# One state-space layer and one attention layer with experts: three orders of work changed, two routings put beside other work

## The reference, cut to what matters

```
xn = layernorm(x)
x  = x + mamba(xn) + one_of_8_experts(xn)          # layer 0
xn = layernorm(x)
x  = x + attention(xn) + two_of_8_experts(xn)      # layer 1
```

```
dt = softplus(dt + dt_bias);  A = -exp(A_log)
L[i,j] = exp(sum of A*dt over j < k <= i), lower triangle only      # the decays within a chunk
y_diag  = (C B^T * L) (x*dt)                                        # within a chunk
S[c+1]  = decay(c) * S[c] + B^T (x*dt*decay to the end of the chunk) # states from chunk to chunk
y_off   = C S[c] * decay from the chunk's start
```

## Time and profile before

| | us |
|---|---|
| median of 3 runs (lowest, highest) | 2052.54 (2051.96, 2064.46) |
| the profiled execution's own time | 2049.56 |
| its span | 2047.8 |
| norm0 | 0 to 49.4 |
| route0 | 50.6 to 69.1 |
| time_steps | 70.1 to 93.3 |
| mamba, before its loop | 94.2 to 133.6 |
| mamba, loop | 133.6 to 716.3 |
| one_expert_each | 720 to 1029 |
| norm1 | 1029.2 to 1092.4 |
| route1 | 1093.6 to 1118.1 |
| project | 1119.1 to 1216 |
| attend_and_experts | 1219 to 2047.8 |

### The profile page before, as it was taken

The page is one execution under the profiler, slowest core; times in us unless marked ns, Lnnn a source line. Parts: engine busy times, 40 slices in busy tenths (PEclk is TensorE's granted clock), DMA queues, the critical chain, the costliest instruction groups (busy, mean ns, idle before and its releaser), DMA issues. The chain is left out here.

```text
span 2047.8 us, 33896 instructions
## 1 busy us (share of the span) xinstructions
PE 1803.0 (88%) x10070; PEld 1240.1 (61%) x10070; DVE 1381.2 (67%) x3090; ACT 1159.0 (57%) x2806; POOL 432.4 (21%) x406
## 2 busy tenths in 40 slices
PE   5389999999999889999844988999999898999998
PEld 2247657656766679999812454555556464656555
DVE  5648678768677612222165869798879888888885
ACT  2145665665565412222111538888888888888886
POOL 2004413422432334321110111020201002020101
PEclk9689899899899889999966999999999999999999
DMA  4412212312221188655173583252424333343311
GB/s 165 137 55 93 92 63 79 105 61 72 92 72 62 42 300 276 201 180 173 54 236 117 159 260 106 73 104 73 104 73 93 63 83 94 83 93 83 86 29 32
DMA packets 143790, 226.12 MB, mean 110 GB/s; under 512 B 17725, under 2 KB 110015, under 8 KB 143648
## 3 DMA queue, kind: packets, MB, share of 16 engines
q1 hardware_dynamic: 124464, 179.95, 29.1%
q0 software_dynamic: 19184, 44.45, 8.5%
HBM read 174.26 MB, written 50.99 MB: 110 GB/s over the span
## 5 line engine op out<-in xcount | busy, mean ns | idle before, releaser
L2286 DVE TENSOR_SCALAR att_scores<-att_psS 128x512 f32<-128x512 f32 x512 | 352.9, 690 | 95.3 <-PE att_psS L2116 94.8
L2235 ACT ACTIVATE att_prob<-att_scores,att_shift 128x512 f32<-128x512 f32 x512 | 383.2, 748 | 23.0 <-DVE att_shift L2302 22.9
L2244 ACT COPY att_pT<-att_psT 128x512 f32<-128x512 f32 x512 | 306.4, 599 | 132.5 <-PE att_psT L2124 131.9
L2294 DVE CUSTOM_DVE_ANT_0 att_scores<-att_scores,first_decay 128x512 f32<-128x512 f32 x512 | 352.0, 688 | 0.0
L2124 PEld LDWEIGHTS att_psT<-ident,att_prob 128*128 128x128 f32 x2048 | 244.8, 142 | 158.7 <-issue 97.6
L2124 PE MATMUL att_psT<-ident,att_prob 128*128 128x128 f32 x2048 | 315.1, 277 | 15.4 <-ACT att_pT L2244 14.8
L2116 PE MATMUL att_psS<-first_ks,first_qs 128*128 128x512 bf16 x512 | 195.8, 384 | 17.3 <-DVE att_scores L2286 13.5
L1123 ACT ACTIVATE mamba_L<-mamba_am,mamba_minus 128x128 f32<-128x128 f32 x512 | 153.9, 387 | 44.5 <-PE mamba_psY L998 44.4
L2138 PE MATMUL att_psO<-att_pT,att_v 128*32 128x512 f32 x1024 | 140.6, 624 | 37.8 <-ACT att_pT L2244 37.8
L1543 ACT ACTIVATE ffn_hT<-ffn_psH,ffn_b 128x128 f32<-128x128 f32 x156 | 44.7, 369 | 194.6 <-PE ffn_psH L1499 194.6
L1499 PEld LDWEIGHTS ffn_psH<-ffn_xT,ffn_w 128*128 128x128 f32 x1248 | 145.3, 192 | 3.6 <-DMA ffn_w<-in_w 0.9
(11 more groups left out here) (287 smaller groups left out, 2872.4 us busy)
## 6 DMA issues: line engine op xcount, KB each, us to landing
ffn_w<-in_w SPq DMA_DIRECT2D x39, 1024.0 KB, 5.6
mamba_am<-a_rows SPq DMA_DIRECT2D x64, 512.0 KB, 3.8
first_qs<-q_parts SPq DMA_DIRECT2D x256, 64.0 KB, 3.1
first_ks<-k_parts SPq DMA_DIRECT2D x256, 64.0 KB, 3.1
xn<-xn_all SPq DMA_DIRECT2D x16, 512.0 KB, 5.7
ffn_w<-in_w POOLq DMA_DIRECT2D x8, 1024.0 KB, 6.7
att_w<-in_inter POOLq DMA_DIRECT2D x7, 1024.0 KB, 5.5
att_w<-in_outer POOLq DMA_DIRECT2D x7, 1024.0 KB, 7.3
```

Of the source, the lines that this page charges most:

```text
L2235: nc.scalar.activation(prob[:, n % NP], scores[:, n % NCL], ACT.Exp, bias=shift[:, h % 2, t:t + 1], accum_out=total[:, octet % 2, t, j, i: ...
L2244: nc.scalar.copy(pT[:, h % HEADS_T, :, t * P:(t + 1) * P], bank_of("turn", n)[:].rearrange("p (k q) -> p k q", k=CPB)).then_inc(pT_ready, 1)
L2286: vec.tensor_scalar(scores[:, n % NCL], psS[n % NS][:], -CLAMP, CLAMP, ALU.max, ALU.min).then_inc(clipped, 1)
L2294: vec.tensor_tensor_reduce(scores[:, n % NCL], scores[:, n % NCL], decay[:, FAR - t * P:FAR - t * P + SEQ], 1.0, -2.0 * CLAMP, ALU.mult, A ...
```

## The change

Four things are changed.

1. **The mamba batch.** DVE's order was decays(0), grow(0), decays(1), grow(1), `fd`, grow(2). It is now grow(0), grow(1), decays(0), `fd`, grow(2), decays(1).
2. **The first table.** Its first two quarters are no longer multiplied ahead of the convolutions; each of the four stands behind a pair of convolutions. `keep_running` has 26 instead of 16 products.
3. **Both routings beside other work.** `route` becomes a class, `Router`, with its pieces as methods. In layer 0 it is merged with `time_steps` into one stage, `route_and_steps`; PE's order has the ranks first, and SP's has the bias and the 8 row stores ahead of `a_rows`. In layer 1 its pieces are spread over the sequences of `project`: b=0 the softmax and the first pick, b=1 the second pick, b=2 the mask (`choose`), b=3 the ranks taken up and `passes`, b=4 both slots and the first one-hot columns, b=5 the second columns and the first one-hot rows, then two quarters of rows per sequence, and the last ones behind the last sequence. On PE the ranks stand behind values(2), one table quarter behind values(6) and seven at the end. The second pick's one-hot rows reuse the first's buffer (semaphore `used`). The latent has one PSUM bank instead of two, so latent(b) waits for ACT's copy of b - 1, which keys(b - 1) ahead of it on PE waits for already.
4. **Row stores of layer 1.** `normalise` stores `xn1` on SP, each sequence behind its store to `out`.

```
-                    decays(0)
                     grow(0)
-                    decays(1)
                     grow(1)
+                    decays(0)
                     dve.wait_ge(fd_done, (i + 1) * CPB)
                     dve.wait_ge(xfd_ready, i * CPB)
                     v.tensor_tensor(fd[:], fd_ps, ...).then_inc(fd_ready, 1)
                     grow(2)
+                    decays(1)
...
-                keep_running(nc, C, psO[0][:, 0:P], 16)
-                for q in range(2):
-                    table.multiply(nc, pe, psP, 0, q)
+                keep_running(nc, C, psO[0][:, 0:P], 26)
...
                 for n in range(CT):
                     conv(0, n, False)
-                    if n in (3, 5):
-                        table.multiply(nc, pe, psP, 0, (n + 1) // 2)
+                    if n % 2 == 1:
+                        table.multiply(nc, pe, psP, 0, n // 2)
...
# normalise, SP
                         sp.dma_start(rows(merge[2], b), x[:, b]).then_inc(x_kept, 16)
+                        sp.wait_ge(xn_ready, (b + 1) * CPB)
+                        sp.dma_start(rows(xn_d, b), xn_all[:, b * CPB:(b + 1) * CPB, :]).then_inc(xn_kept, 16)
...
# route_and_steps, DVE
                 v.scalar_tensor_tensor(out=mag[:], ...).then_inc(mag_ready, 1)
+                router.chained(dve)
+                router.shift(dve)
                 dve.wait_ge(exped, 2)
                 v.tensor_scalar(w[:], u[:], 1.0, None, ALU.add).then_inc(w_ready, 1)
+                router.probabilities(dve)
+                router.pick(dve, 0)
+                router.choose(dve)
                 dve.wait_ge(w_ready, 1)
...
                            op0=ALU.mult, op1=ALU.mult).then_inc(a_ready, 1)
+                router.rank_all(dve)
+                router.tiles_of(dve)
+                router.first_slots(dve)
                 dve.wait_ge(decay_ready, 1)
...
# project, SP
                 sp.dma_start(wuv[:], w["wuv"]).then_inc(w_in, 16)
+                router.load(sp)
                 first.load_wo(sp)
# project, PE
                 def latent(b):
-                    if b >= 2:
-                        pe.wait_ge(lat_ready, b - 1)
+                    pe.wait_ge(lat_ready, b)
...
                     values(b)
-                pe.wait_ge(lat_ready, BATCH - 1)
-                for k in range(2):
-                    for q in range(4):
-                        table.multiply(nc, pe, psL[0][:, 0:2 * table.columns], k, q)
+                    if b == 2:
+                        router.ranks(pe)
+                    elif b == BATCH - 2:
+                        table.multiply(nc, pe, psR[:, 0:2 * table.columns], 0, 0)
+                for q in range(1, 4):
+                    table.multiply(nc, pe, psR[:, 0:2 * table.columns], 0, q)
+                for q in range(4):
+                    table.multiply(nc, pe, psR[:, 0:2 * table.columns], 1, q)
# project, DVE
                 v.tensor_tensor(wkT[:], wkT[:], wvT[:], ALU.add).then_inc(joined, 1)
+                router.chained(dve)
+                router.shift(dve)
                 dve.wait_ge(wkv_made, 1)
...
                         take_low(Q, b - 1)
+                    if b == 1:
+                        router.pick(dve, 1)
+                    elif b == 3:
+                        router.rank_all(dve)
+                    elif b == 4:
+                        router.second_slots(dve, 0)
+                    elif b == 5:
+                        table.columns_hot(nc, dve, choice, 1)
+                    elif b > 5:
+                        quarter = 2 * (b - 5) - 1
+                        table.rows_hot(nc, dve, choice, quarter // 4, quarter % 4)
                     if b < BATCH:
                         take(K, b)
                         subtract(Q, b)
                     if b:
                         take_low(K, b - 1)
-                    if b < 2:
-                        table.columns_hot(nc, dve, choice, b)
-                    if b < BATCH:
-                        table.rows_hot(nc, dve, choice, b // 4, b % 4)
-                table.take(nc, dve, psL[0], places)
+                    if b == 0:
+                        router.probabilities(dve)
+                        router.pick(dve, 0)
+                    elif b == 2:
+                        router.choose(dve)
+                    elif b == 3:
+                        router.passes(dve)
+                    elif b == 4:
+                        router.second_slots(dve, 1)
+                        table.columns_hot(nc, dve, choice, 0)
+                    elif b > 4:
+                        quarter = 2 * (b - 5)
+                        table.rows_hot(nc, dve, choice, quarter // 4, quarter % 4)
+                table.rows_hot(nc, dve, choice, 1, 3)
+                table.take(nc, dve, psR, places)
```

354 lines of the change are left out of this document (190 added, 164 removed).

## The result

Four runs of the changed kernel have a median of 2028.93 us (2023.86 to 2032.48), against 2053.05 for the kernel before: ratio 0.9858, 95% interval 0.9826 to 0.989. That is 24 us faster where I had forecast 57, and above my range. The kernel before moved too, from 2053.05 beside the first set to between 2038.02 and 2041.68 beside the others, so only the ratios compare across sets, and these two agree within their intervals. The profiled execution took 2028.95, its span is 2026.6.

What follows compares the result with a forecast made beforehand. Mamba's loop was taken as bound by PE, busy 550.4 of 582.7 us at mean clock 0.94, gaining where PE waits. Terms 28 + 13 + 4.5 + 11.5 = 57 off 2049.56 gave 1992.6, plus 3.0: 1995.5 us, range 1976 to 2023.

Steps and rivals of the forecast that it cites:

- The mamba batch: Mamba loop: DVE's earlier copies remove PE's 2.88 us wait per sequence and the low clock behind it; -28 (-10 to -38).
- the sign of being wrong that I had named: Mamba loop: a PE wait before diagonal(1) of 2 us or more would show the prediction wrong.
- Rival A: Mamba: lead lost between DVE and POOL, L(1) late, PE waits some 3 us, clock falls later; -4 to -16; chance 0.25.
- Route0 and time_steps: Layer 0's two short stages merged: DVE's chain ends at 79.9 instead of 93.3; -13 (-11 to -14).
- The first table: Mamba's start: table quarters between pairs of convolutions, last convolution ending at 121.6 instead of 126.06; -4.5 (-2 to -7).
- the lower end that I had named: First table at mamba's start: only -2 if the weights land late and PE idles into the low clock.
- Layer 1: Layer 1's routing stage goes (-25.5), row stores hide in norm1, project gets 14 longer; -11.5.
- project's lengthening: Project: router pieces on DVE, the later bias and shift, and low clock after PE's idle 3.1 add +14 (+10 to +19).
- Rival C: Layer 1 gives nothing back: project grows by 25, DVE waiting for PE in sequences 5 to 7; time 2007; chance 0.13.
- all good ends together: Whole kernel: every step at its best gives -73, 1979.
- the forecast: The forecast's own case: mamba -20 to -38 and layer 1 -6 to -15; chance 0.55.
- Rivals B and D: B: slower, PE idles in mamba's dense part, 2055 to 2075, chance 0.04. D: copies not earlier, mamba 0, 2023, chance 0.03.

Runs made afterwards that it cites:

- pool_quiet: Changed kernel with POOL's products beside the third growth and first decays cut to one head of eight: 2004.66 us (one run), mamba loop 562.9.
- wait_filled: Changed kernel with eight products without use on PE behind diagonal(0), filling its wait for L(1): 1993.04 us, ratio 0.9767 to the kernel before, loop 545.9.
- again: The changed kernel run once more, unaltered: 2009.19 us, ratio 0.9836 to the kernel before.
- ranks_later: Changed kernel with PE's ranks in project behind queries(3) instead of values(2): 2004.26 us, ratio 0.9807 to the kernel before, project 115.7.
- table_warm: Changed kernel with 6 and 12 products without use filling PE's waits ahead of project's last table quarters: 2006.51 us, ratio 0.9819 to the kernel before.
- grow2_last: Changed kernel with DVE's order grow(0), grow(1), fd, decays(0), decays(1), grow(2): 2005.93 us, ratio 0.9824 to the kernel before, loop 558.9.
- no_wait: grow2_last with POOL's xdt(1) ahead of xfd(0): 2007.40 us, ratio 0.9815 to the kernel before, loop 557.4.
- skip_v2: Changed kernel with PE's skip matmuls of tile 1 moved between diagonal(0) and diagonal(1): 2018.69 us, ratio 0.989 to the kernel before, loop 563.8.
- skip_v1: no_wait with PE's skip matmuls of tile 1 moved behind diagonal(1), ahead of its state product: 2007.82 us, ratio 0.9846 to the kernel before, loop 559.1.

## Why the prediction was wrong

**The mamba batch, forecast -28, measured -13: this step failed.** Its first half was right: the wait of 2.88 went, PE made its second growth 3 us sooner. The second half read "waits about 0.7 for L(1)" and added "if it stays at full clock". The wait was 2.1 (0.5 to 0.7 by my own times), the sign of being wrong that I had named. PE came to diagonal(0) when I had said, 15.0 behind `near` for 15.2. But L(1) came at 19.1, not at 17.6, of which the stretch beside POOL is 1.3 (1.17 and 1.03 for 0.68 each, 1.71 for 1.23; pool_quiet took back the last two). And I took it that a wait so short would not touch the clock, with no row to show it. Rival A had this: L(1) late, PE waiting before diagonal(1), the clock falling "as before, only later", mamba -4 to -16. I gave it 0.25. wait_filled, where L(1) is as late as before and only the fill and the clock differ, shows that the clock is the missing half: with it held the loop gains 28.3. What A had too high is the share of the stretch: in pool_quiet, with 0.8 us of it taken away, the wait is as long, and by its rows some 1.4 of the 2.1 would stand with no stretch at all.

The Trainium skill (SBUF — State Buffer, "Who interferes with whom") has the later of the two operations wait until the other is done. The trace agrees nearly: L(0) starts at 208.55 while POOL's `xdt` (208.14, 1.04 us) has 0.63 to go, and takes 0.48 longer than alone.

**Route0 and time_steps, -13, measured -14.4.** Right: DVE's chain was the bound, as counted. **The first table, -4.5, measured -4.4** in the first profile (39.3 from the stage's start to the first z product, then 34.9), and -2.5 in `again` (36.8). The order of things was right. The full size was met only in the five profiles of fifteen with the slow `keep_running`, which is luck; the ten others went by the lower end that I had named, the weights landing late and PE idling into the low clock.

**Layer 1, -11.5, measured -4.6** (the mean of the first profile and `again`; -5.5 over ten profiles). Norm1 took no longer, the stores were hidden as said. The term mis-sized is project's lengthening, +14, measured +22.8. Up to sequence 3 it was nearly right: the wait was 3.1, and DVE had the queries of sequence 3 at 8.8 later than before, where my terms (1, 4.1 and 2.5 for the clock) make 7.6. What failed comes behind. I allowed nothing for the clock at the end, but the last four quarters of the table ran at half clock, since PE waits there for one-hot rows that DVE, being the bound, brings late: DVE then waits 7.2 us for the table where I had 1.8. And I counted DVE's split at 6.94 throughout, but four of its rows are stretched beside POOL's `valued`, 4 us in all (1.82 and 2.71, 1.73 and 2.72, for 1.21 each). ranks_later gave back 7.0, near to what I had priced for the wait and the clock behind it (4.1 and 2.5), and table_warm 4.4 of the 5.4 at the end, of which about 2 reached the attention. Rival C's time for this stage (25 longer) was nearly met, but not by its mechanism: from the ranks on DVE has one long wait for PE, 7.7 us for the queries right behind them, and none over a microsecond until the table is out.

**The sums.** Three figures of the prediction don't come out of its own terms: the router's pieces are 18.1, not 18.4; all good ends together are about -74, not -73; and the chances of the forecast and the four rivals add up to 1.00, so that nothing was unassigned and "faster by over 1%" should have had 0.96. None of them bears on what failed.

**What I left out.** The hole in one_expert_each, 16 us of the profiled execution, had no part in the reasons. Without it the profiled execution would have been near 2013, inside the range, but that would have been no merit of the reasons: with the ratio of `again` the gain is 33 of the 57, and the mamba step falls short by the same half.

Rivals B and D did not happen: the loop is shorter, and the copies come right behind PE's first growth (202.59, 1.1 us behind its start).

## What to carry to other kernels

Where a reorder removes a wait of TensorE, ask which wait takes its place, and price the clock behind it as well as the wait: here 2.1 us of waiting per sequence cost another 1.6 us (13.1 over eight) in low clock. If the new wait can't be removed, filling it with products without use gave back 13 us here. Four orders that shortened, moved or split the wait (grow2_last, no_wait, skip_v2, skip_v1) gave the loop nothing, and not for one reason: in grow2_last the clock fell behind 0.97 us all the same, in no_wait DVE set the pace, and in skip_v2 the clock held but an earlier TensorE moved POOL's products onto DVE's next L. So after such an edit look for the next wait before you judge it by the time. An order of POOL's that keeps its products off the decays was not tried.

And where work is spread over a stage until another engine becomes its bound, what that engine makes last meets a TensorE that has begun to wait: the last four quarters of the table took 13.90, and 7.34 with the waits filled.
